# Causal linear attention on one core: scores of two sequences in one 64x64 tile, with block-diagonal keys written by ScalarE and V moved by 8 DMAs a step

## The reference, cut to what matters

```python
xn = layernorm(x)
q, k, v = heads(xn @ Wq.T + bq), heads(xn @ Wk.T + bk), heads(xn @ Wv.T + bv)
q = softmax(exp(beta) * q, axis=-1)          # over the 8 channels of a head
k = softmax(exp(beta) * k, axis=-1)
kv = cumsum(einsum('zsD,zsd->zsDd', k, v), axis=1)
kn = cumsum(k, axis=1)
out = einsum('zsD,zsDd->zsd', q, kv) / sum(q * kn, axis=-1)
x + out @ Wo.T + bo + (fp8_rounded(xn / input_scale) * input_scale) @ (weight_fp8 * weight_scale).T + bias
```

## Time and profile before

| | |
|---|---|
| median of 3 runs | 1386.97 us (1383.36 to 1387.37) |
| the profiled execution | 1375.45 us |
| its span, first to last instruction | 1373.7 us |
| instructions in it | 81313 |
| mean granted clock of TensorE | 0.967 |
| PE busy, matmuls | 1224.7 us, 89% |
| DVE busy | 1024.7 us, 75% |
| ACT busy | 577.5 us, 42% |
| POOL busy | 321.5 us, 23% |
| DMA engines busy | 30.3% on the main queue, 77 GB/s |

### The profile page before, as it was taken

How to read it: one execution, slowest core, us unless ns; L and a number is a source line. 1 busy time by engine, 2 the same in 40 slices (tenths; PEclk the granted TensorE clock), 3 DMA queues, 4 the chain that set the end, 5 groups by cost and what they waited for, 6 DMA issues and landing times.

```text
span 1373.7 us, 81313 instructions
## 1 busy us (share of the span) xinstructions
PE 1224.7 (89%) x36322; PEld 731.5 (53%) x36322; DVE 1024.7 (75%) x2031; ACT 577.5 (42%) x1049; POOL 321.5 (23%) x590
## 2 busy tenths in 40 slices
PE   1569999998999999999999899999999999999995
PEld 1335555555555555555555555555555555555653
DVE  4667778877777887778777777877777877778872
ACT  1534344444444444444444344344344444344431
POOL 3132222222222222222222222221222222122210
PEclk8789999999999999999999999999999999999998
DMA  8022232323323333333333333233233333323321
GB/s 223 10 67 65 75 84 75 82 76 79 75 73 83 70 85 76 81 74 85 76 75 77 76 80 71 77 79 69 76 86 66 76 86 77 75 77 76 69 65 42
DMA packets 181142, 106.01 MB, mean 77 GB/s; under 512 B 120160, under 2 KB 153056, under 8 KB 180832
## 3 DMA queue, kind: packets, MB, share of 16 engines
q1 hardware_dynamic: 180112, 99.79, 30.3%
q10 hardware_dynamic: 720, 1.31, 0.6%
HBM read 40.20 MB, written 16.78 MB: 41 GB/s over the span
## 4 chain that ended last, share of the span: by engine, by line
PE 86%; issue 8%; DVE 2%; DMA 1%; SPq 1%; POOL 0%; ACT 0%; POOLq 0%; DVEq 0%; ACTq 0%
PE s_ps L888 10%; PE a_ps L985 7%; PE a_ps L1004 6%; PE a_ps L905 6%; PE k_ps L861 5%; PE vo_ps L861 5%; PE vo_ps L963 5%; PE vo_ps L863 4%; PE k_ps L865 4%; PE vo_ps L865 4%; PE k_ps L863 4%; PE vo_ps L872 4%; PE vo_ps L874 4%; PE vo_ps L876 4%; PE q_ps L863 4%
## 5 line engine op out<-in xcount | busy, mean ns | idle before, releaser
L507 ACT ACTIVATE q_heads<-qT,cst 128x512 f32<-128x512 f32 x256 | 164.0, 711 | 88.1 <-DVE qT L753 88.1
L400 POOL TENSOR_TENSOR y_sum<-y,y_magic 128x512 f32<-128x512 f32 x64 | 81.4, 1272 | 450.3 <-DVE y_magic L614 450.3
L659 DVE TENSOR_TENSOR att<-s_ps,cst 128x512 f32<-128x512 f32 x256 | 163.8, 681 | 2.1 <-PE s_ps L888 2.1
L393 POOL TENSOR_TENSOR x_split<-xn,x_split 128x512 f16<-128x512 f32 x64 | 74.0, 1157 | 370.6 <-ACT x_split L455 363.4
L498 ACT ACTIVATE q_e<-q_shift,q_exp_scale 128x512 f32<-128x512 f32 x64 | 46.2, 722 | 252.0 <-DVE q_shift L632 252.0
L888 PE MATMUL s_ps<-q_heads,kT 32*32 32x128 f32 x8192 | 148.3, 272 | 2.1 <-issue 1.2
L888 PEld LDWEIGHTS s_ps<-q_heads,kT 32*32 32x32 f32 x8192 | 113.6, 103 | 56.3 <-issue 56.3
L985 PE MATMUL a_ps<-st_seqs,q_heads 128*32 128x36 f32 x8192 | 99.3, 201 | 35.6 <-issue 33.9
L712 DVE TENSOR_TENSOR vp<-vo_ps,vp 128x512 f32<-128x512 f32 x64 | 44.3, 692 | 109.1 <-PE vo_ps L865 109.1
L985 PEld LDWEIGHTS a_ps<-st_seqs,q_heads 128*32 128x32 f32 x8192 | 89.1, 109 | 68.4 <-issue 66.1
L905 PE MATMUL a_ps<-vp,k_e 32*32 32x36 f32 x8064 | 115.0, 198 | 6.4 <-issue 6.3
(11 more groups left out here) (136 smaller groups left out, 2450.4 us busy)
## 6 DMA issues: line engine op xcount, KB each, us to landing
v_groups<-vp SPq DMA_DIRECT2D x1024, 18.0 KB, 2.4
x_in<-L_attn_x SPq DMA_DIRECT2D x64, 256.0 KB
x_res<-L_attn_x SPq DMA_DIRECT2D x64, 256.0 KB
out<-o_sb SPq DMA_DIRECT2D x64, 256.0 KB
w_own<-L_attn_Wk SPq DMA_DIRECT2D x1, 1024.0 KB, 11.4
w_own<-L_attn_Wq SPq DMA_DIRECT2D x1, 1024.0 KB, 13.5
w_own<-L_attn_Wv SPq DMA_DIRECT2D x1, 1024.0 KB, 15.2
att<-L_ffn_weight_fp SPq DMA_DIRECT2D x1, 1024.0 KB, 16.9
```

The source lines that it names most:

```text
L393: gp.tensor_tensor(x_split[:, 1, :], xn[:, :], x_split[:, 0, :], ALU.subtract)\
L400: gp.tensor_tensor(y_sum[:, :], y[:, :], y_magic[:, :], ALU.add).then_inc(ysum_ready, 1)
L507: last = sc.activation(q_heads[:, i.parity, :, j, :], qT[:, :, :], ACT.Copy, scale=head_mask[:, j:j + 1])
L659: v.tensor_tensor(att[:, c, :, :, :].rearrange("p g j s -> p (g j) s"), s_ps[:, DM * (c % 2):DM * (c % 2 + 1)].rearrange("p (h s) -> p h s ...
```

## The change

Two sequences now share a tile. ScalarE writes each step's keys twice into `k_pairs`, once for each sequence of a pair with the channels of the other sequence's partitions set to zero (`pair_mask`). The weights of a scores product are then 64 rows (two sequences x 32 channels) by 64 columns (two sequences x 32 tokens), block-diagonal, in a 64x64 tile of the array; 32 products a step take the place of 64. `kT` loses its second buffer, `k_pairs` has two. `att` and `v_groups` are laid out so that partitions 32 (2 gp + c) to 32 (2 gp + c) + 31 belong to group 2 q + gp and sequence 2 n + c, and V reaches its place by 8 DMAs a step of twice the size. Heads of a group are numbered to suit (`v_head`, and the order in which the rows of Wv are turned). The products at L1004 stay 64 a step with the same shapes, and DVE's operations keep theirs.

```diff
--- before.py
+++ after.py
@@ -37,7 +37,8 @@
 HEADS = 64
 DH = DM // HEADS
 J = 4
-GL = 4
+GP = 2
+SP = 2
 G = HEADS // J
 KC = DM // P
 STEPS = LEN // TOK
@@ -61,7 +62,8 @@
 C_ID = 0
 C_HEAD = C_ID + P
 C_SEQ = C_HEAD + J
-C_TRI = C_SEQ + SEQS
+C_PAIR = C_SEQ + SEQS
+C_TRI = C_PAIR + SP
 C_ALL = C_TRI + TOK
 
 class Step:
@@ -137,6 +139,7 @@
         ident = cst[:, C_ID:C_ID + P]
         head_mask = cst[:, C_HEAD:C_HEAD + J]
         seq_mask = cst[:, C_SEQ:C_SEQ + SEQS]
+        pair_mask = cst[:, C_PAIR:C_PAIR + SP]
         tri = cst[:, C_TRI:C_TRI + TOK]
         w_hi = sb("w_hi", [P, MATRICES, KC, DM], F16)
         w_lo = sb("w_lo", [P, MATRICES, KC, DM], F16)
@@ -188,10 +191,11 @@
         k_e = sb("k_e", [P, 2, DM])
         vp = sb("vp", [P, 2, HEADS, VW])
         qT = sb("qT", [P, G, TOK])
-        kT = sb("kT", [P, 2, G, TOK])
+        kT = sb("kT", [P, G, TOK])
+        k_pairs = sb("k_pairs", [P, 2, G, SP, TOK])
         q_heads = sb("q_heads", [P, 2, G, J, TOK])
-        v_groups = sb("v_groups", [P, 2, GL, SEQS, G // GL, J, VW])
-        att = sb("att", [P, SEQS, G // GL, J, TOK])
+        v_groups = sb("v_groups", [P, 2, GP * SP, SEQS // SP, G // GP, J, VW])
+        att = sb("att", [P, SEQS // SP, G // GP, J, TOK])
         st_masked = sb("st_masked", [P, G, J, VW])
         st_step = sb("st_step", [P, G, VW])
         st_run = sb("st_run", [P, G, VW])
@@ -251,6 +255,7 @@
         ksum_ready, krec_ready, vp_ready = sem("ksum_ready"), sem("krec_ready"), sem("vp_ready")
         qT_ready, kT_ready = sem("qT_ready"), sem("kT_ready")
         qheads_ready, v_cleared = sem("qheads_ready"), sem("v_cleared")
+        kpairs_ready = sem("kpairs_ready")
         v_moved = [[sem(f"v_moved{n}_{b}") for b in range(SEQS)] for n in range(2)]
         scores_done, att_ready = sem("scores_done"), sem("att_ready")
         state_done, masked_ready, ststep_ready = sem("state_done"), sem("masked_ready"), sem("ststep_ready")
@@ -303,9 +308,10 @@
                 if t.after(2):
                     sp.wait_ge(a_done, (t - 1).n)
                 for b in range(SEQS):
-                    for gl in range(GL):
-                        sp.dma_start(v_groups[TOK * gl:TOK * (gl + 1), t.parity, gl, b],
-                                     vp[TOK * b:TOK * (b + 1), t.parity, HEADS // GL * gl:HEADS // GL * (gl + 1)])\
+                    for gp in range(GP):
+                        to = SP * gp + b % SP
+                        sp.dma_start(v_groups[TOK * to:TOK * (to + 1), t.parity, to, b // SP],
+                                     vp[TOK * b:TOK * (b + 1), t.parity, HEADS // GP * gp:HEADS // GP * (gp + 1)])\
                             .then_inc(v_moved[t.parity][b], 16)
 
             def turn_x(t):
@@ -492,6 +498,13 @@
                 if last_weights:
                     last_weights()
                 if i.exists():
+                    act.wait_ge(kT_ready, (i + 1).n)
+                    if i.after(2):
+                        act.wait_ge(scores_done, (i - 1).n * 2)
+                    for c in range(SP):
+                        last = sc.activation(k_pairs[:, i.parity, :, c, :], kT[:, :, :], ACT.Copy,
+                                             scale=pair_mask[:, c:c + 1])
+                    last.then_inc(kpairs_ready, 1)
                     act.wait_ge(qshift_ready, (i + 1).n)
                     if i.after(1):
                         act.wait_ge(qT_ready, i.n)
@@ -656,7 +669,8 @@
             def mask_scores(t, c):
 
                 dve.wait_ge(scores_done, t.n * 2 + c // 2 + 1)
-                v.tensor_tensor(att[:, c, :, :, :].rearrange("p g j s -> p (g j) s"),
+                v.tensor_tensor(att[:, c % 2, 4 * (c // 2):4 * (c // 2) + 4, :, :]
+                                .rearrange("p g j s -> p (g j) s"),
                                 s_ps[:, DM * (c % 2):DM * (c % 2 + 1)].rearrange("p (h s) -> p h s", s=TOK),
                                 tri[:, None, :].to_broadcast([P, 4 * J, TOK]), ALU.mult)\
                     .then_inc(att_ready, 1)
@@ -689,11 +703,13 @@
                 if i.after(2):
                     dve.wait_ge(state_done, (i - 1).n * 2)
                     for b in range(SEQS):
-                        dve.wait_ge(v_moved[i.parity][b], i.half * 16 * GL)
-                v.reciprocal(vp[:, i.parity, :, DH].rearrange("p (l q j) -> p q l j", l=GL, j=J),
-                             k_sum[:, :].rearrange("p (q l j) -> p q l j", l=GL, j=J))\
+                        dve.wait_ge(v_moved[i.parity][b], i.half * 16 * GP)
+                v.reciprocal(vp[:, i.parity, :, DH].rearrange("p (l q j) -> p q l j", l=GP, j=J),
+                             k_sum[:, :].rearrange("p (q l j) -> p q l j", l=GP, j=J))\
                     .then_inc(krec_ready, 1)
-                v.transpose(kT[:, i.parity].rearrange("p g s -> p (g s)"), k_e[:, i.parity, :])\
+                if i.after(1):
+                    dve.wait_ge(kpairs_ready, i.n)
+                v.transpose(kT[:, :, :].rearrange("p g s -> p (g s)"), k_e[:, i.parity, :])\
                     .then_inc(kT_ready, 1)
 
             def output(t):
@@ -853,7 +869,7 @@
 
             def v_head(g):
 
-                return J * (G // GL * (g % GL) + g // GL)
+                return J * (G // GP * (g % GP) + g // GP)
 
             def project(bank, t, m, seeded):
 
@@ -877,17 +893,17 @@
                               skip_group_check=rest)
                 return last
 
-            def scores(t, pair):
+            def scores(t, half):
 
                 pe.sem_inc(pe_waited, 1)
-                for gq in range(G // GL):
-                    for gl in range(GL):
-                        for n in range(2):
-                            b = 2 * pair + n
-                            rows = slice(TOK * b, TOK * (b + 1))
-                            last = mm(s_ps[TOK * gl:TOK * (gl + 1), DM * n + P * gq:DM * n + P * (gq + 1)],
-                                      kT[rows, t.parity, GL * gq + gl, :],
-                                      q_heads[rows, t.parity, GL * gq + gl, :, :], start=True, stop=True)
+                for q in range(4):
+                    for gp in range(GP):
+                        g = GP * (4 * half + q) + gp
+                        for n in range(SEQS // SP):
+                            rows = slice(SP * TOK * n, SP * TOK * (n + 1))
+                            last = mm(s_ps[SP * TOK * gp:SP * TOK * (gp + 1), DM * n + P * q:DM * n + P * (q + 1)],
+                                      k_pairs[rows, t.parity, g, :, :].rearrange("p c s -> p (c s)"),
+                                      q_heads[rows, t.parity, g, :, :], start=True, stop=True)
                 last.then_inc(scores_done, 1)
 
             def state(t, n):
@@ -913,7 +929,7 @@
                     project(k_ps, i, MK, seeded=True).then_inc(k_done, 1)
                 t = i - 1
                 if t.exists():
-                    pe.wait_ge(kT_ready, (t + 1).n)
+                    pe.wait_ge(kpairs_ready, (t + 1).n)
                     pe.wait_ge(qheads_ready, (t + 1).n)
                     if t.after(1):
                         pe.wait_ge(att_ready, t.n * 4)
@@ -994,15 +1010,15 @@
                 if t.exists():
                     pe.wait_ge(att_ready, (t + 1).n * 4)
                     for b in range(SEQS):
-                        pe.wait_ge(v_moved[t.parity][b], (t + 2).half * 16 * GL)
+                        pe.wait_ge(v_moved[t.parity][b], (t + 2).half * 16 * GP)
                     pe.sem_inc(pe_waited, 1)
-                    for gq in range(G // GL):
-                        groups = a_ps[:, a_col(GL * gq):a_col(GL * gq) + GL * GW]\
-                            .rearrange("p (g b w) -> p b g w", g=GL, w=VW)
-                        for b in range(SEQS):
+                    for q in range(G // GP):
+                        groups = a_ps[:, a_col(GP * q):a_col(GP * q) + GP * GW]\
+                            .rearrange("p (g n w) -> p n g w", g=GP, w=SP * VW)
+                        for n in range(SEQS // SP):
                             for j in range(J):
-                                last = mm(groups[TOK * j:TOK * (j + 1), b], att[:, b, gq, j, :],
-                                          v_groups[:, t.parity, :, b, gq, j, :], start=False, stop=True,
+                                last = mm(groups[TOK * j:TOK * (j + 1), n], att[:, n, q, j, :],
+                                          v_groups[:, t.parity, :, n, q, j, :], start=False, stop=True,
                                           skip_group_check=True)
                     last.then_inc(a_done, 1)
 
@@ -1020,7 +1036,7 @@
                         src = (wo_sorted if m == MO else w_nat[m])[:, oc, c * P:(c + 1) * P]
                         dst = bank_of(n)[:, oc * P:(oc + 1) * P]
                         if m == MV:
-                            dst = bank_of(n).rearrange("p (l q f) -> p q l f", l=GL, q=G // GL)[:, oc]
```

(2 more changed lines are left out.)

## The result

The changed kernel takes 1306.96 us (median of 4 runs, 1303.11 to 1313.17) against 1385.16 us before (4 runs, 1381.10 to 1387.37): ratio 0.9447, 95% interval 0.9404 to 0.9490, 78 us or 5.5% faster. The forecast was 1352 with a range of 1326 to 1388.

A forecast was written before the change was run, and what follows sets the result against it. It took short steps as paced by DVE in a PE–DVE loop, long ones as held by late PE instruction packets. Surplus −38.6 and switches +4 us gave −34.6, from 1386.97 to 1352.4 us; range 1326 to 1388.

The forecast's parts named there:

- Scores on PE: Scores call: 32 matmuls on 4 places still take 0.98 us, plus 0.1 to 0.2 us for the tile-shape switch.
- (a): Rival at the scores: a call gets short, 0.49 us, 21 us more gain, 1331 us; chance 0.09.
- (b): Rival at the scores: 64×64 tiles slower, 1.96 us a call at twice the time, 1435 us; chance 0.12.
- PE's stream: PE's instruction queue: 1021 instructions a step, not 1149; packet breaks drift by 3 a step, surplus falls 38.6 us.
- (c): Rival on PE's holes: not a matter of packets, or they return elsewhere; nothing gained, 1387 us; chance 0.08.
- (d): Rival on PE's stream: breaks start elsewhere through miscounted waits; surplus 35 to 100 us, 1334 to 1399; chance 0.09.
- 13 × 3.0 = 39 us: Surplus of steps up to 14, breaks at the end of L985, start of v and end of L1004.
- 8 × 1.8 = 14 us: Surplus of steps from 16 or so to 23, a break in the k projection right behind L1004.
- +4 us for switches: In the 21 long steps PE sets the pace, and the two tile-shape switches cost 0.2 us a step.
- ScalarE: Two masked copies, 1.42 us a step, 91 us busy in all; q_e moves by 0.15 us, hidden with 1 us over.
- SP and DMA: Eight fewer moves of V free 5.8 us of SP a step, xT issued earlier; nothing gains, counted at nothing.
- I am wrong if short steps change by over 0.3 us: Sign against the forecast: short steps, about 18.6 us, should not themselves change by over 0.3 us.

The follow-up runs named there:

- dma16_only: The changed kernel with V moved by 16 DMAs of 18 KB a step as before, nothing else; 1335.46 us.
- lock_good: The changed kernel plus 132 spare TensorE instructions (satisfied waits) in the set-up and three in each step, holding the phase of short steps 40 to 45; 1274.14 us.
- lock_bad: As lock_good, but 237 spare instructions in the set-up in place of 132, holding the phase of long steps 7 and 8; 1464.79 us.
- act_double: lock_q with two more ScalarE copies of k_exp in each step, into a tile nobody reads; 1261.03 us.
- tiny_dmas: lock_q with two more DMAs of 32 bytes a step, issued on SP's queue when the output projection has ended; 1274.24 us.
- pad128: The changed kernel with 128 spare TensorE instructions in each step, eight ahead of each group of k, q and output projection matmuls; 1797.11 us.
- lock_q: lock_good with each step's three spare instructions moved from the head of the k projection into the middle of the q projection; 1260.78 us.
- shift190: The changed kernel with 190 spare TensorE instructions once in the set-up and none in the steps; 1283.00 us.
- lock_dma16: lock_good with V moved by 16 DMAs of 18 KB a step instead of 8 of 36 KB; 1294.82 us.

## Why the prediction was wrong in size

*Scores on PE*: right. A call takes 1.03 us, 0.05 over the 0.98, where I had put 0.1 to 0.2 within bounds of nothing and 0.4. Rivals (a), 0.49 us, and (b), over 1.3 us, are both refuted, though (b)'s load is real: 133 ns for 64 columns against 103, so 30 ns more and not the 13 that I had worked out. With SP's issuing as before, a short step kept its length to 0.07 us (dma16_only).

*PE's stream*: the mechanism was right and is now shown by lock_good against lock_bad, which refutes rival (c); (d) fell too, since the breaks stand at the predicted instructions from step 3 on; that step 2 had none is a matter of whether the packet was late, which the prediction took for given. The profile called these holes "issue" and the Trainium skill (Runtime: NRT & Kernel Launch, Instruction fetch mechanics) calls the cost of a block boundary mostly hidden; by that rule the two kernels would differ by nothing, and they differ by 191 us. Of the two terms, 13 × 3.0 = 39 us measured 38.5 (steps 3 to 15, 275.6 us less 13 × 18.24), and 8 × 1.8 = 14 us measured 6.0 (steps 17 to 22, 115.4 less 6 × 18.24). The second was mis-sized: I priced holes in the k projection by six steps of the old kernel, three of which (19, 21 and 62) had a second hole in the first half of the state (L905), one packet on, and a fourth (17) one in L1004; in the new stream the next break lies behind the q projection, and that hole is gone. The +4 us for switches in the long steps isn't seen either. Together 12.6 us too little gain.

*ScalarE*, and DVE's work: right. ACT is 83.5 us busier, for the 91 forecast, q_e starts 10.2 us into the step around 706 us as it did into the one around 712 us before, and act_double shows that the cover is larger than I said.

*SP and DMA: "Nothing gains"*: this is the step that failed, a term put at nothing that measured 28.5 us (dma16_only against the changed kernel). Without it the forecast's 1352 stood against 1335.5, inside the range. I noted that 8 fewer moves free 5.8 us of SP's queue and that xT is issued earlier, and then asked only who waits for xT. Nobody does. But the issuing itself had stood beside L985. Moving it away shortened the state burst (first to last 1.25 us at the median of dma16_only's steps, 1.10 in the changed kernel) and took away pauses in the second burst and a late packet in step 1: 20 us between the profiled steps of the two (1177.0 and 1157.1), 28.5 us in the medians. The hint was there: in the kernel before, L1004, the same 128 matmuls of the same shape, has windows of 1.11 to 1.13 us from first to last start in eight steps, and L985 of 1.22 to 1.45 in the four of them in which it has no hole. I didn't compare them, and took the 18.59 us of a short step for a floor that DVE sets. It is none: the burst itself lies in the loop of PE and DVE, behind PE's wait for the masks, and tiny_dmas makes it 0.20 us longer and every step 0.20 us longer. "I am wrong if short steps change by over 0.3 us" is what came true, at 0.35, but only just: some 0.04 of it is the different cut of short steps, and some 0.05 that 19 of the 27 short steps of before were even ones, 22 of 42 after, and even ones are some 0.25 us longer.

The account for the profiled executions, whose steps fell by 68.3 us against 34.6 forecast: 12.6 from the surplus, 21 from the short steps, together 34 of the 34 missing. That split is arithmetic; by the runs, the steps of dma16_only are 48.4 us under those before, 13.8 more than forecast, and the DMAs bring the other 19.9. The range had no lower end for the DMAs at all; a bound from the row of the burst, 61 × 0.2 to 0.4 us, would have reached 1328.

## What to carry to other kernels

In an unrolled stream of many small matmuls the place of a 256-instruction boundary can be worth more than the work: count the instructions of a step modulo 256, look for a hole that drifts by a fixed count, and try a few spare instructions in a cheap place before tuning the work; a change that alters the count must be compared at its best phase, or it is judged by luck. Here at good phases the changed kernel has 1260.8 us. The changed kernel as it stands has its gain in part by luck: its 1021 instructions a step leave the bad places at step 23, and at lock_bad's phase the same work takes 1464.8 us, more than before. And ask of every transfer not only who waits for it, but what the issuing queue runs beside.

## What was not expected of the hardware

Two DMAs of 32 bytes issued while TensorE starts 128 fp32 loads and matmuls of 32 and 36 columns stretch that burst from 1.10 to 1.30 us, by one or two pauses of some 0.1 us. A spare instruction of two satisfied waits costs some 0.08 us of PE's time at the head of a projection (lock_good, three: 0.24), about 0.09 each in a row of eight ahead of every fp8-weight matmul and 0.03 each in a row of eight ahead of every third projection matmul (pad128), and nothing when three stand behind projection matmuls (lock_q). And a step whose only fault is a late packet can be 22 to 23 us long, not 21, where the hole brings a stretch at TensorE's lower level: in shift190's step 52 eight v matmuls start 0.43 us apart and not 0.22, 1.2 GHz for 2.4. Its window (us, busy by engine, granted clock, DMA share, GB/s):

```profile
1014.38:1036.90 22.52, 20.01 (x512) 11.12 (x504) 15.80 (x33) 10.08 (x19) 6.05 (x15) 0.92 0.33 85
```

All these numbers are of this stream. No run shows how the new scores do at the old length of the stream. How much of the DMAs' 28.5 us is pauses in bursts and how much late packets is known for the profiled executions only as far as the split under dma16_only tells; at the good phase the DMAs are worth 20.7 us (lock_dma16), and two small DMAs beside the burst alone 13.5 us (tiny_dmas).
